# Deeper buffer rings and a new order of all engines in a pre-norm attention and FFN kernel

## The chip, the cores and the metric

The kernel runs on one core of a Trainium2 chip. The metric is device time in microseconds (us). The kernel before took 173.91 us (median of three runs, 173.37 to 174.36). The core's engines are TensorE (PE, with its weight load PEld), VectorE (DVE), ScalarE (ACT) and GpSimd (POOL); SyncE (SP) issues nearly all DMAs.

## The reference

The input x is (32, 256, 128) in float32: 32 sequences of 256 rows, 128 features, 8 heads of 16. One layer is computed:

```
h  = layernorm(x)
q, k, v, g = h @ Wq.T, h @ Wk.T, h @ Wv.T, h @ Wg.T
q, k = rope(q), rope(k)
kv, ksum, vsum = sum_s k_s v_s, sum_s k_s, sum_s v_s     # per head
num = (q @ kv) * scale + vsum;  den = (q . ksum) * scale + S
o  = num / den + depthwise_conv5(v) + bias               # conv over s
x2 = x + (o * g) @ Wo.T
h2 = layernorm(x2) in bfloat16, divided by s_in, rounded to fp8 e4m3
out = x2 + (h2_fp8 @ W_fp8) * (s_in * s_k) + ffn_bias
```

## The kernel before

The work is cut into 16 units (U) of two sequences each, that is 512 rows as four tiles of 128 (TPU). Every unit goes through the same stages, and each engine executes its share in an order that is written out by hand, one call per stage and unit; so several units are in flight at once, and an engine that waits for one stage holds up whatever stands behind it in its own list. Ordering between engines is by counting semaphores: a stage waits for its inputs, and for the reader of the buffer that it overwrites.

The path of one unit u:

- SP `load_x`: x from HBM into `xs` (256 KB, a ring of NX = 4 units). It waits until `residual(u - 4)` has read the slot.
- DVE `stats1`, ACT `var_eps1`, POOL `pow1`, ACT `norm1`: the first layer norm, giving `h`. PE `transpose_h`, ACT `move_hT`: its transpose `hT`.
- PE `project_q`, `project_k`, `project_v`, `project_g` (L1260, L1269, L1279, L1287) from hT. DVE `turn_q_unit` (L968) and `turn_k_unit` (L980) multiply q and k by cosines and sines. SP `swap_q` (L271, L272) moves the two halves of q across partitions with two DMAs, and POOL `add_q` (L700) adds, giving `qT`. POOL `add_k` (L707) gives `k`.
- ACT `move_v`, PE `transpose_v`, ACT `conv_middle` and `conv_outer`, DVE `conv_tap` three times (L995), POOL `sum_outer`: the convolution in `acc`.
- PE `key_value` (L1305), DVE `mask_kv` (L1006), PE `sum_v` and `attend` (L1324), DVE `invert` and `divide`, PE `transpose_t1` (L1333), DVE `add_lepe` (L1030) and `gate`, PE `project_o` (L1343), DVE `residual` (L1047) giving `x2`.
- DVE `stats2`, ACT `var_eps2`, POOL `pow2`, ACT `norm2` (L451): `h2` in bfloat16. SP `turn_h2` (L279) transposes it by DMA into `h2T`; ACT `quantise_if_small` (L485) makes `q8`, PE `ffn` (L1385), ACT `move_y`, POOL `add_bias` and `final_sum`, SP `store` (L261). Units 14 and 15 use PE for this transpose.

q, k, v and the other products live in eight PSUM banks that stages share in turns. A PE stage names in its call which reader must have freed its bank; `project_v(1, (q_turned_done, count(0)))` waits until the DVE has read q of unit 0 from the same bank.

Units 5 to 11 run through regular loops (on the DVE `for t in range(5, 12)`, on PE `for t in range(7, 13)`); the first and the last units have orders of their own. SP has one queue, and its list mixes loads, swaps, transposes and stores, each behind its own wait. Three lines decide what is said of it below:

```
if u >= NX: sp.wait_ge(x2_done, count_last(u, NX))      # load_x
sp.wait_ge(q_turned_done, count(u))                     # swap_q
sp.wait_ge(h2_done, count(u))                           # turn_h2
```

Of the kernel before, what the change touches and what calls it, by code (L numbers as in the profile page):

```python
# [5 lines left out]
P = 128  # L6
D = 128
# [15 lines left out]
NX = 4  # L23
# [33 lines left out]
def h2T_count(u):  # L57

    return 16 * (u // 2 + 1)
# [10 lines left out]
def build(nc, x, wq, wk, wv, wg, wo, lepe_w, lepe_b, ffn_w, s_in, s_k, ffn_b,  # L70
          turn_q_c, turn_k_c, ident_c, mask_c, out):
    ctx = ExitStack()
    with ctx:
# [43 lines left out]
        q_turned = sb("q_turned", [P, 2, 2, W])  # L117
        q_swapped = sb("q_swapped", [P, 2, W])
        k_turned = sb("k_turned", [P, 2, TPU, 2, D])
        k = sb("k", [P, 2, TPU, 2, D // 2])  # L120
        v = sb("v", [P, 3, TPU, NW])
        qT = sb("qT", [P, 2, W])
# [8 lines left out]
        x2 = sb("x2", [P, 3, TPU, D])  # L131
# [5 lines left out]
        h2 = sb("h2", [P, 2, TPU, D], BF16)  # L137
        h2T = sb("h2T", [P, 2, W], BF16)
# [4 lines left out]
        ob = sb("ob", [P, 2, TPU, D])  # L143
# [7 lines left out]
        p_kv = bank[4][:, 0:BPU * NW].rearrange("p (j e) -> p j e", j=BPU)  # L151
        p_h2T = bank[2][:, 0:W // 2].bitcast(BF16)
        p_hT = bank[3]
        p_proj = bank[5][:].rearrange("p (t d) -> p t d", t=TPU)
        p_gT = bank[5]
        p_vT = bank[2][:].rearrange("p (j s) -> p j s", j=BPU)
        p_t1T = bank[3]
        p_y = bank[0]
        p_first_hT = [b[:, 0:S] for b in (bank[2], bank[0])]
        p_end_h2T = [b[:, 0:S // 2].bitcast(BF16) for b in (bank[0], bank[1])]  # L160
        p_end_y = [b[:, 0:S].rearrange("p (t d) -> p t d", t=TPB) for b in (bank[5], bank[4])]
        p_end_t1T = [b[:, 0:S] for b in (bank[4], bank[1])]
        p_end_gT = [b[:, 0:S] for b in (bank[5], bank[3])]
        p_end_proj = [b[:, 0:S].rearrange("p (t d) -> p t d", t=TPB) for b in (bank[0], bank[1])]
# [10 lines left out]
        ob_free = [sem(f"ob_free{n}") for n in range(2)]  # L175
# [27 lines left out]
        q_swapped_in = [sem(f"q_swapped_in{n}") for n in range(2)]  # L203
# [26 lines left out]
        h2T_in = [sem(f"h2T_in{n}") for n in range(2)]  # L230
# [18 lines left out]
        def _(sp):  # L249
# [7 lines left out]
            def store(u):  # L257
                if not 0 <= u < LAST:
                    return
                sp.wait_ge(ob_done, count(u))  # L260
                sp.dma_start(out_v[u], ob[:, u % 2]).then_inc(ob_free[u % 2], 16)  # L261

            def store_end(j):
                sp.wait_ge(end_ob_done[j], 1)
                half = slice(TPB * j, TPB * (j + 1))
                sp.dma_start(out_v[LAST][:, half], ob[:, LAST % 2, half]).then_inc(ob_free[LAST % 2], 16)

            def swap_q(u):
                s = u % 2
# [4 lines left out]
            def turn_h2(u):  # L274
                s = u % 2
# [24 lines left out]
            load_x(3)  # L300
            swap_q(0)
            swap_q(1)
            load_x(4)
# [3 lines left out]
            load_x(5)  # L307
            turn_h2(1)
            for t in range(6, 7):
                load_x(t)  # L310
                swap_q(t - 2)
                turn_h2(t - 4)
                store(t - 5)
            load_x(7)
            store(0)
            swap_q(5)
            turn_h2(3)
            load_x(8)
            store(2)
            swap_q(6)  # L320
            turn_h2(4)
            load_x(9)
            swap_q(7)
            turn_h2(5)
            store(4)
            load_x(10)
            swap_q(8)
            store(3)
            turn_h2(6)
            load_x(11)  # L330
            store(5)
            swap_q(9)
            turn_h2(7)
            store(6)
            swap_q(10)
            load_x(12)
            turn_h2(8)
            swap_q(11)
            store(7)
            load_x(13)  # L340
            turn_h2(9)
            load_x(14)
            swap_q(12)
            load_x(15)
            swap_q(13)
            store(8)
            turn_h2(10)
            turn_h2(11)
            swap_q(14)
            store(9)  # L350
# [10 lines left out]
            sp.wait_ge(ob_free[0], 16 + 16 * (U // 2))  # L361
            sp.wait_ge(ob_free[LAST % 2], 16 + 16 * (U // 2) + 16)

        @block.scalar
        def _(act):
# [79 lines left out]
            def norm2(u):  # L445
                s = u % 2
                act.wait_ge(nmr2_done, count_last(u))
                if u >= 2:
                    act.wait_ge(h2T_in[s], h2T_count(u - 2))
                for t in range(TPU):  # L450
                    last = nc.scalar.activation(h2[:, s, t], x2[:, u % 3, t], ACT.Identity, scale=rs2[:, s, t:t + 1],  # L451
# [3 lines left out]
            def end_norm2():  # L455
                s = LAST % 2
                act.wait_ge(nmr2_done, count_last(LAST, j=0))
                act.wait_ge(h2T_in[s], h2T_count(LAST - 2))
                for t in range(TPB):
                    last = nc.scalar.activation(h2[:, s, t], x2[:, LAST % 3, t], ACT.Identity,  # L460
# [17 lines left out]
            def quantise_if_small(u, is_small):  # L478
                with act.If(is_small == 1):
                    if u < PE_H2:  # L480
                        act.wait_ge(h2T_in[u % 2], h2T_count(u))
# [3 lines left out]
                    nc.scalar.activation(q8[:, u % 2], h2T[:, u % 2] if u < PE_H2 else p_h2T, ACT.Copy, scale=rsc[:, 0:1],  # L485
# [14 lines left out]
            move_hT(0, 1)  # L500
            var_eps1(1)
            move_v(0)
            var_eps1(2)
            norm1(1)
            conv_outer(0)
            conv_middle(0)
            move_hT(1)
            var_eps1(3)
            move_v(1)
            norm1(2)  # L510
            move_hT(2)
            conv_outer(1)
            conv_middle(1)
            norm1(3)
            move_hT(3)
            move_v(2)
            conv_outer(2)
            conv_middle(2)
            var_eps2(0)
            var_eps1(4)  # L520
            move_v(3)
            norm2(0)
            norm1(4)
# [8 lines left out]
            norm2(1)  # L532
            move_v(4)
            var_eps1(5)
            conv_middle(4)
            conv_outer(4)
            quantise_if_small(1, is_small)
            norm1(5)
# [3 lines left out]
            norm2(2)  # L542
            move_v(5)
            var_eps1(6)
            conv_middle(5)
            conv_outer(5)
            quantise_if_small(2, is_small)
            norm1(6)
            var_eps2(3)
            move_y(2)  # L550
            move_hT(6)
            norm2(3)
            move_v(6)
            var_eps1(7)
            conv_middle(6)
            conv_outer(6)
            quantise_if_small(3, is_small)
            norm1(7)
            var_eps2(4)
            move_y(3)  # L560
            move_hT(7)
            norm2(4)
            move_v(7)
            var_eps1(8)
            conv_middle(7)
            conv_outer(7)
            quantise_if_small(4, is_small)
            norm1(8)
            round_identity()
            var_eps2(5)  # L570
            move_y(4)
            move_hT(8)
            for t in range(9, 12):
# [9 lines left out]
                move_hT(t)  # L583
            norm2(8)
            move_v(11)
            var_eps1(12)
            conv_outer(11)
            conv_middle(11)
            quantise_if_small(8, is_small)
            norm1(12)  # L590
# [3 lines left out]
            var_eps1(13)  # L594
            norm2(9)
            norm1(13)
            move_hT(13)
            move_v(12)
            quantise_if_small(9, is_small)
            var_eps2(10)  # L600
            var_eps1(14)
# [991 lines left out]
```

## Time and profile before

| | |
|---|---|
| median of three runs | 173.91 us |
| profiled execution: its own time | 173.71 us |
| its span, first to last instruction | 171.9 us |
| PE busy | 153.9 us (90%) |
| DVE busy | 150.1 us (87%) |
| POOL busy | 136.3 us (79%) |
| ACT busy | 126.3 us (73%) |
| DMA queue of SP and ACT | 33.9% of 16 DMA engines |

The span is 1.81 us shorter than the profiled execution's own time. An engine is busy from the start of an instruction to its end, overlaps counted once; the rest of the span it waits. A row of the timeline gives the start, the duration (of one, or of the merged run when it says x2 or more), the engine, the line, and what is written and read; in square brackets stands the idle time just before it and who ended it.

### The profile page before, as it was taken

How to read it: one execution, taken by the hardware profiler on the slowest of the kernel's cores; microseconds unless marked ns; L12 is line 12 of the kernel's file. 1: busy time of each engine (PE TensorE's matmuls, PEld its weight loads, DVE VectorE, ACT ScalarE, POOL GpSimd, SP SyncE). 2: the span in 40 equal slices, each digit the busy share in tenths (PEclk: the TensorE clock that was granted, in tenths of full speed). 3: DMA queues.
4: the chain of work that ended last, by engine and by line, in shares of the span. 5: the costliest groups of instructions: out<-in, count | busy, mean ns of one | idle time of the engine just before them, and what ended most of it. 6: DMA issues, size and time to landing. Idle time of an engine off the chain costs nothing.

```text
span 171.9 us, 3695 instructions
## 1 busy us (share of the span) xinstructions
PE 153.9 (90%) x1052; PEld 124.9 (73%) x1052; DVE 150.1 (87%) x281; ACT 126.3 (73%) x342; POOL 136.3 (79%) x163
## 2 busy tenths in 40 slices
PE   7789999999899999979999999997999799987620
PEld 2378898877688888858887989857787587965400
DVE  2279899999999999978999999969999959999663
ACT  3757783697889888598889798856798686583851
POOL 1436988858989999969889898969499796979970
PEclk9999999999999999999999999999999999999985
DMA  4932022133133616131552552341508050323223
GB/s 126 280 84 61 4 63 80 44 63 95 31 122 95 185 31 185 34 122 34 153 124 68 144 128 74 72 131 36 123 2 214 5 129 26 97 60 93 66 64 114
DMA packets 29286, 15.74 MB, mean 92 GB/s; under 512 B 9680, under 2 KB 26960, under 8 KB 29264
## 3 DMA queue, kind: packets, MB, share of 16 engines
q1 hardware_dynamic: 28688, 15.22, 33.9%
q10 hardware_dynamic: 576, 0.26, 0.6%
q8 instruction: 9, 0.15, 0.4%
q14 instruction: 13, 0.11, 0.2%
HBM read 5.25 MB, written 4.19 MB: 55 GB/s over the span
## 4 chain that ended last, share of the span: by engine, by line
DVE 23%; PE 22%; DMA 17%; issue 14%; POOL 10%; SPq 7%; ACT 5%; DVEq 0%; POOLq 0%; ACTq 0%
DMA xs<-_attn_hidden_states_dram 6%; DVE acc L995 6%; DMA h2T<-h 5%; DMA q_swapped<-q_turned 5%; DVE k_turned L980 4%; PE bank L1305 4%; DVE x L1047 3%; PE bank L1287 3%; DMA w_raw<-in_L_attn_Wo_dram 3%; POOL rs L671 3%; PE bank L1279 3%; DVE st L958 2%; ACT h L451 2%; PE bank L1269 2%; POOL ob L730 2%
## 5 line engine op out<-in xcount | busy, mean ns | idle before, releaser
L995 DVE SCALAR_TENSOR_TENSOR acc<-bank,conv_w,acc 128x510 f32<-128x510 f32 (+1 forms) x48 | 34.7, 722 | 0.1
L393 ACT ACTIVATE h<-xs,nmr,rs 128x128 f32<-128x128 f32 x64 | 26.3, 483 | 1.7 <-POOL nmr L663 1.5
L451 ACT ACTIVATE h<-x,nmr,rs 128x128 bf16<-128x128 f32 x60 | 24.7, 482 | 3.9 <-POOL nmr L674 3.3
L660 POOL TENSOR_TENSOR rs<-ve,minus_half 128x4 f32<-128x4 f32 (+1 forms) x17 | 16.7, 981 | 10.0 <-ACT ve L384 10.0
L671 POOL TENSOR_TENSOR rs<-ve,minus_half 128x4 f32<-128x4 f32 (+1 forms) x17 | 16.6, 978 | 8.7 <-ACT ve L442 8.6
L700 POOL TENSOR_TENSOR qT<-q_turned,q_swapped 128x512 f32<-128x512 f32 x16 | 20.4, 1277 | 3.4 <-DMA q_swapped<-q_turned 3.4
L1343 PEld LDWEIGHTS bank<-w_o,oT 128*128 128x128 f32 x128 | 16.3, 191 | 7.8 <-issue 4.0
L707 POOL TENSOR_TENSOR k<-k_turned 128x512 f32<-128x512 f32 x16 | 20.4, 1275 | 1.8 <-DVE k_turned L980 1.8
L716 POOL TENSOR_TENSOR acc<-acc,outer 128x508 f32<-128x508 f32 x16 | 20.3, 1271 | 0.6 <-DVE acc L995 0.6
L980 DVE TENSOR_TENSOR k_turned<-bank,turn_k 128x1024 f32<-128x1024 f32 x16 | 19.5, 1218 | 1.3 <-PE bank L1269 1.3
L1305 PEld LDWEIGHTS bank<-v,k 128*128 128x128 f32 x128 | 16.6, 190 | 4.4 <-issue 2.9
L968 DVE TENSOR_TENSOR q_turned<-bank,turn_q 128x1024 f32<-128x1024 f32 x16 | 19.4, 1215 | 0.1
L1343 PE MATMUL bank<-w_o,oT 128*128 128x128 f32 x128 | 17.4, 277 | 2.3 <-DVE oT L1039 2.3
L723 POOL TENSOR_TENSOR yc<-yb,fb 128x512 bf16<-128x512 bf16 x15 | 17.4, 1158 | 1.4 <-ACT yb L492 1.4
L1279 PE MATMUL bank<-w_v,hT 128*128 128x128 f32 x128 | 17.2, 277 | 1.0 <-ACT hT L405 0.7
L1324 PEld LDWEIGHTS p_num<-kvs,qT 128*128 128x128 f32 x128 | 16.8, 190 | 1.7 <-POOL qT L700 0.8
L1305 PE MATMUL bank<-v,k 128*128 128x136 f32 x128 | 17.8, 282 | 0.0
L730 POOL TENSOR_TENSOR ob<-x,yc 128x512 f32<-128x512 f32 x15 | 17.4, 1162 | 0.4
L1279 PEld LDWEIGHTS bank<-w_v,hT 128*128 128x128 f32 x128 | 15.7, 192 | 2.8 <-issue 1.6
L1324 PE MATMUL p_num<-kvs,qT 128*128 128x136 f32 x128 | 17.6, 279 | 0.0
L1316 PE MATMUL p_num<-w_v,hsum 128*128 128x272 f32 x64 | 17.4, 394 | 0.1
L1287 PE MATMUL bank<-hT,w_g 128*128 128x512 f32 (+1 forms) x34 | 16.8, 576 | 0.5 <-DVE x L1047 0.4
(90 smaller groups left out, 338.3 us busy)
## 6 DMA issues: line engine op xcount, KB each, us to landing
q_swapped<-q_turned SPq DMA_DIRECT2D x32, 128.0 KB, 2.8
xs<-_attn_hidden_states_dram SPq DMA_DIRECT2D x15, 256.0 KB, 3.2
out_dram<-ob SPq DMA_DIRECT2D x15, 256.0 KB, 2.9
xs<-_attn_hidden_states_dram SPq DMA_DIRECT2D x2, 128.0 KB, 2.8
turn_q<-in_turn_q_dram SPq DMA_DIRECT2D x1, 256.0 KB, 4.1
turn_k<-in_turn_k_dram SPq DMA_DIRECT2D x1, 256.0 KB, 4.3
out_dram<-ob SPq DMA_DIRECT2D x2, 128.0 KB, 1.8
h2T<-h SPq DMA_TRANSPOSE x14, 2.4
```

The source lines that it names most:

```text
L393: last = nc.scalar.activation(h[:, s, t], xs[:, u % NX, t], ACT.Identity, scale=rs1[:, s, t:t + 1], bias=nmr1[:, s, t:t + 1])
L451: last = nc.scalar.activation(h2[:, s, t], x2[:, u % 3, t], ACT.Identity, scale=rs2[:, s, t:t + 1], bias=nmr2[:, s, t:t + 1])
L671: nc.gpsimd.tensor_tensor(rs2[:, s, part], ve2[:, s, part], minus_half[:, part], ALU.pow).then_inc(pow2_done, 1)
L700: nc.gpsimd.tensor_tensor(qT[:, s], q_turned[:, s, 0], q_swapped[:, s], ALU.add).then_inc(qT_done, 1)
L730: nc.gpsimd.tensor_tensor(ob[:, s], x2[:, u % 3], yc[:, s], ALU.add).then_inc(ob_done, 1)
L980: nc.vector.tensor_tensor(k_turned[:, s].rearrange("p (j a) h d -> p j a h d", j=BPU), p_k.rearrange("p (j a) d -> p j a d", j=BPU).unsque ...
L995: nc.vector.scalar_tensor_tensor(out=part, in0=p_vT[:, :, lo + off:hi + off], scalar=conv_w[:, k:k + 1], in1=part, op0=ALU.mult, op1=ALU.a ...
L1279: last = nc.tensor.matmul(p_v[:, t], hT[:, u % 3, t * P:(t + 1) * P], w_v[:, 0:D], start=True, stop=True)
L1287: nc.tensor.matmul(p_gT[:] if j is None else p_end_gT[j], w_g[:], hT[:, u % 3, part_of(j)], start=True, stop=True).then_inc(gT_filled, 1)
L1305: last = nc.tensor.matmul(p_kv[:, t // TPB], k[:, u % 2, t].rearrange("p a d -> p (a d)"), v[:, u % 3, t], start=(t % TPB == 0), stop=(t % ...
L1324: last = nc.tensor.matmul(p_num[:, t, 0:NW], qT[:, u % 2, t * P:(t + 1) * P], kvs[:, u % 2, t // TPB], start=False, stop=(t % TPB == TPB - 1))
L1343: last = nc.tensor.matmul(dst[:, n], oT[:, u % 2, t * P:(t + 1) * P], w_o[:], start=True, stop=True)
```

## The change

Buffers: `xs` grows from 4 to 6 slots, `x2` from 3 to 4, and `q_turned`, `q_swapped`, `k`, `qT`, `h2`, `h2T` and `ob` from 2 to 3. The waits that protect a slot look back as many units further. PSUM banks are dealt out anew: k, v and the FFN's product share one bank (before: q, v and the FFN's product); q shares one with the transposes of h (before: the transpose of t1 shared that one); kv, the transpose of v and the transpose of t1 have a bank each.

The orders of all five engines are new. In the regular loop little moves: PE projects q before k, and the DVE turns q before k, where it was k before q. The first five units and the last five have other orders. No arithmetic is added or removed.

```diff
-NX = 4
+NX = 6
-        q_turned = sb("q_turned", [P, 2, 2, W])
+        q_turned = sb("q_turned", [P, 3, 2, W])
...
-        p_q = bank[0]
-        p_k = bank[1][:].rearrange("p (t d) -> p t d", t=TPU)
+        p_q = bank[3]
+        p_k = bank[0][:].rearrange("p (t d) -> p t d", t=TPU)
...
             def turn_h2(u):
-                s = u % 2
+                s = u % 3
                 sp.wait_ge(h2_done, count(u))
-                if u >= 2:
-                    sp.wait_ge(q8_done, count(u, 2))
+                if u >= 3:
+                    sp.wait_ge(q8_done, count(u, 3))
...
             def add_k(u):
                 s = u % 2
                 pool.wait_ge(k_turned_done, count(u))
-                if u >= 2:
-                    pool.wait_ge(kv_filled, count(u, 2))
+                if u >= 3:
+                    pool.wait_ge(kv_filled, count(u, 3))
...
# PE, regular loop
-                transpose_t1(t - 3, (hT_done, count_first(t - 1)))
+                transpose_t1(t - 3, (t2_done, count_last(t - 4)))
                 project_v(t - 1, (yb_done, count(t - 5)))
-                project_k(t - 1, (k_turned_done, count(t - 2)))
+                project_q(t - 1, (hT_done, count_first(t - 1)))
                 transpose_v(t - 1, (tap_done[-1], count(t - 2)))
-                project_q(t - 1, (v_done, count(t - 1)))
+                project_k(t - 1, (v_done, count(t - 1)))
...
-                ffn(t - 4, is_small, (q_turned_done, count(t - 1)))
-                transpose_h(t, (t2_done, count_last(t - 3)))
+                ffn(t - 4, is_small, (k_turned_done, count(t - 1)))
+                transpose_h(t, (q_turned_done, count(t - 1)))
```

The first place is PE at the start of the program, from the first projection of k or q on. The rows before (one projection of q is L1260, of k L1269, of v L1279, of g L1287; the transposes of v, h are L1295, L1252; L1305 is key_value, L1316 sum_v):

```order
L1269 MATMUL bank<-w_qk,hT 128x128 x4
L1260 MATMUL bank<-hT,w_qk 128x512
L1316 MATMUL p_num<-w_v,hsum 128x2x136 x2
L1295 MATMUL bank<-ident,v 128x128 x4
L1287 MATMUL bank<-hT,w_g 128x512
L1252 MATMUL bank<-ident,h 128x128 x4
L1305 MATMUL bank<-v,k 128x136 x4
L1279 MATMUL bank<-w_v,hT 128x128 x4
L1269 MATMUL bank<-w_qk,hT 128x128 x4
```

And now (the same functions stand 15 lines further down: q L1275, k L1284, v L1294, g L1302; transposes of v, h L1310, L1267; key_value L1320, sum_v L1331):

```order
L1275 MATMUL bank<-hT,w_qk 128x512
L1310 MATMUL bank<-ident,v 128x128 x4
L1284 MATMUL bank<-w_qk,hT 128x128 x4
L1331 MATMUL p_num<-w_v,hsum 128x2x136 x2
L1302 MATMUL bank<-hT,w_g 128x512
L1267 MATMUL bank<-ident,h 128x128 x4
L1284 MATMUL bank<-w_qk,hT 128x128 x4
L1320 MATMUL bank<-v,k 128x136 x4
L1275 MATMUL bank<-hT,w_qk 128x512
L1294 MATMUL bank<-w_v,hT 128x128 x4
```

Unit 0's q and its transpose of v now stand ahead of its k; unit 1's k ahead of key_value of unit 0, and unit 1's v last, where it was ahead of unit 1's k.

The second place is SP's queue around the loads of the last units. Before, from the load of x for unit 13 to the transposes of h2 for units 10 and 11 (the three loads are units 13, 14 and 15; the transposes 9, then 10 and 11; the swaps 12 and 13; the store 8):

```order
L255 DMA xs<-in_L_attn_hidden_states_dram 128x4x128
L279 DMA_TRANSPOSE h2T<-h 128x4x128
L255 DMA xs<-in_L_attn_hidden_states_dram 128x4x128
L271 DMA q_swapped<-q_turned 64x512
L272 DMA q_swapped<-q_turned 64x512
L255 DMA xs<-in_L_attn_hidden_states_dram 128x4x128
L271 DMA q_swapped<-q_turned 64x512
L272 DMA q_swapped<-q_turned 64x512
L261 DMA out_dram<-ob 128x4x128
L279 DMA_TRANSPOSE h2T<-h 128x4x128 x2
```

And now, from the transpose of unit 8 to that of unit 10 (transposes 8, 9 and 10; swaps 11, 12 and 13; the load of unit 15; stores 7 and 8):

```order
L279 DMA_TRANSPOSE h2T<-h 128x4x128
L271 DMA q_swapped<-q_turned 64x512
L272 DMA q_swapped<-q_turned 64x512
L255 DMA xs<-in_L_attn_hidden_states_dram 128x4x128
L261 DMA out_dram<-ob 128x4x128
L271 DMA q_swapped<-q_turned 64x512
L272 DMA q_swapped<-q_turned 64x512
L279 DMA_TRANSPOSE h2T<-h 128x4x128
L261 DMA out_dram<-ob 128x4x128
L271 DMA q_swapped<-q_turned 64x512
L272 DMA q_swapped<-q_turned 64x512
L279 DMA_TRANSPOSE h2T<-h 128x4x128
```

The loads have moved up: those of units 13 and 14 now stand ahead of this piece, unit 15's ahead of the swap of unit 12, and between the transpose of unit 9 and that of unit 10 there is no load any more; with six slots they wait for x2 of units 7, 8 and 9 where they waited for 9, 10 and 11.

## Rows read from the trace of the kernel before

**Rows 1.** Stretches: start:end, length, then busy us of each engine
```profile
core 0: us, PE busy (x) PEld busy (x) DVE busy (x) ACT busy (x) POOL busy (x), PEclk, DMA share, GB/s
...
60.00:70.00 10.00, 10.00 (x77) 8.84 (x76) 9.96 (x20) 8.74 (x25) 9.54 (x11) 1.00 0.33 93
20.00:110.00 90.00, 87.70 (x625) 74.44 (x624) 87.83 (x156) 74.17 (x200) 79.59 (x90) 1.00 0.34 91
110.00:160.00 50.00, 45.52 (x316) 36.96 (x314) 44.14 (x85) 34.43 (x93) 41.40 (x45) 1.00 0.35 86
160.00:172.00 12.00, 3.25 (x24) 1.94 (x24) 6.82 (x13) 5.58 (x15) 6.21 (x8) 0.75 0.26 74
```

**Rows 2.** DVE timeline, one unit of the regular loop
```profile
59.20 0.68 DVE L1030 TENSOR_TENSOR t<-bank,acc 128x512 f32<-128x512 f32 x1
...
62.28 1.23 DVE L968 TENSOR_TENSOR q_turned<-bank,turn_q 128x1024 f32<-128x1024 f32 x1
...
68.00 0.68 DVE L1030 TENSOR_TENSOR t<-bank,acc 128x512 f32<-128x512 f32 x1
```

**Rows 3.** PE timeline, the same unit
```profile
58.98 1.06 PE L1279 MATMUL bank<-w_v,hT 128*128 128x128 f32 x8
...
61.22 1.02 PE L1260 MATMUL bank<-hT,w_qk 128*128 128x512 f32 x2
```

**Rows 4.** DVE timeline: the larger waits after 70 us, and q_turned of unit 13
```profile
77.84 0.44 DVE L1006 TENSOR_TENSOR kvs<-bank,mask 128x272 f32<-128x272 f32 x1 [1.32 <-PE bank L1305]
...
114.55 0.76 DVE L958 BATCH_NORM_STATS2 st<-xs 128x6 f32<-128x256 f32 x2 [1.43 <-DMA xs<-_attn_hidden_states_dram]
...
122.88 0.76 DVE L958 BATCH_NORM_STATS2 st<-xs 128x6 f32<-128x256 f32 x2 [0.41 <-DMA xs<-_attn_hidden_states_dram]
123.56 1.21 DVE L968 TENSOR_TENSOR q_turned<-bank,turn_q 128x1024 f32<-128x1024 f32 x1
...
139.90 0.69 DVE L1047 TENSOR_TENSOR x<-bank,xs 128x512 f32<-128x512 f32 x1 [1.25 <-PE bank L1343]
141.27 0.19 DVE L1012 TENSOR_SCALAR den<-p_num 128x32 f32<-128x32 f32 x1 [0.67 <-PE p_num L1324]
```

**Rows 5.** SP's queue, 111 to 138 us
```profile
111.36 0.55 SPq L255 DMA_DIRECT2D xs<-_attn_hidden_states_dram  x1
...
128.38 0.38 SPq L255 DMA_DIRECT2D xs<-_attn_hidden_states_dram  x1
128.80 0.52 SPq L271 DMA_DIRECT2D q_swapped<-q_turned  x1
...
130.00 0.60 SPq L261 DMA_DIRECT2D out_dram<-ob  x1
130.70 7.96 SPq L279 DMA_TRANSPOSE h2T<-h  x2
```

**Rows 6.** ACT timeline: waits for the transposed h2, and norm2 of unit 10
```profile
73.05 0.72 ACT L485 ACTIVATE q<-h2T,rsc 128x512 fp8e4<-128x512 bf16 x1 [1.48 <-DMA h2T<-h]
...
127.55 1.64 ACT L451 ACTIVATE h<-x,nmr,rs 128x128 bf16<-128x128 f32 x4
...
134.87 0.72 ACT L485 ACTIVATE q<-h2T,rsc 128x512 fp8e4<-128x512 bf16 x1 [2.10 <-DMA h2T<-h]
```

**Rows 7.** All transposes of h2, from issue to landing
```profile
DMA to landing us min/median/max: 2.4/2.4/4.1
```

**Rows 8.** PE timeline at the start
```profile
15.79 1.16 PE L1279 MATMUL bank<-w_v,hT 128*128 128x128 f32 x8
...
19.59 0.60 PE L1252 MATMUL bank<-ident,h 128*128 128x128 f32 x4
```

**Rows 9.** DVE timeline at the start
```profile
11.39 1.23 DVE L980 TENSOR_TENSOR k_turned<-bank,turn_k 128x1024 f32<-128x1024 f32 x1
...
17.88 1.23 DVE L980 TENSOR_TENSOR k_turned<-bank,turn_k 128x1024 f32<-128x1024 f32 x1 [0.83 <-PE bank L1269]
...
31.39 0.74 DVE L995 SCALAR_TENSOR_TENSOR acc<-bank,conv_w,acc 128x510 f32<-128x510 f32 x1
```

More of the change, by code:

```diff
@@ L541, in _ @@
             move_y(1)
[L542 to L573, printed above, removed]
+            for t in range(6, 9):
                 norm2(t - 4)
@@ L736, in _ @@
             pow1(2)
+            pow1(3)
             add_q(0)
-            pow1(3)
             add_k(1)
@@ L762, in _ @@
             sum_outer(4)
[L763 to L777 removed]
+            for t in range(7, 12):
                 add_k(t - 2)
@@ L1107, in _ @@
             invert(2)
+            stats1(5)
+            divide(2)
             conv_tap(3, 1)
-            divide(2)
+            mask_kv(3)
+            add_lepe(2)
             conv_tap(3, 2)
-            for t in range(5, 12):
+            gate(2)
+            turn_q_unit(4)
+            turn_k_unit(4)
+            quantise_if_wide(1, is_small)
+            residual(2)
+            conv_tap(4, 0)
+            stats2(2)
+            invert(3)
+            conv_tap(4, 1)
+            divide(3)
+            conv_tap(4, 2)
+            for t in range(6, 11):
                 mask_kv(t - 2)
@@ L1476, in _ @@
+            project_k(11, (v_done, count(11)))
+            transpose_v(11, (tap_done[-1], count(10)))
+            project_o(9, (oT_done, count_last(9)))
+            sum_v(10, (t1_done, count_last(9)))
+            transpose_h(12, (q_turned_done, count(11)))
+            attend(10)
+            ffn(8, is_small, (k_turned_done, count(11)))
             project_g(10, (x2_done, count_last(9)))
+            project_q(12, (hT_done, count_first(12)))
             key_value(11, (kvs_done, count(10)))
-            transpose_t1(10, (hT_done, count_first(12)))
+            project_v(12, (yb_done, count(8)))
@@ L1485, in _ @@
[L1485 to L1492 removed]
+            project_k(13, (k_turned_done, count(12)))
+            key_value(12, (kvs_done, count(11)))
@@ L1493, in _ @@
+            project_q(13, (hT_done, count_first(13)))
+            transpose_t1(11, (t2_done, count_last(10)))
+            sum_v(12, (t1_done, count_last(11)))
+            ffn(9, is_small, (k_turned_done, count(13)))
+            attend(12)
+            project_g(11, (x2_done, count_last(10)))
+            project_v(13, (yb_done, count(9)))
+            transpose_h(14, (q_turned_done, count(13)))
             project_o(11, (oT_done, count_last(11)))
-            sum_v(12, (t1_done, count_last(11)))
@@ L1495, in _ @@
-            project_v(13, (yb_done, count(9)))
-            transpose_h(14, (t2_done, count_last(11)))
-            attend(12)
+            key_value(13, (kvs_done, count(12)))
             transpose_v(13, (tap_done[-1], count(12)))
-            project_q(14, (v_done, count(13)))
+            transpose_t1(12, (t2_done, count_last(11)))
+            sum_v(13, (t1_done, count_last(12)))
+            ffn(10, is_small, (v_done, count(13)))
             project_g(12, (x2_done, count_last(11)))
-            project_k(14, (k_turned_done, count(13)))
```

570 lines of the change are left out of this document (299 added, 271 removed).

## Prediction

> **What bounds the kernel now.** I read the stretches first, then one unit of the loop on the DVE and on PE, then the waits inside the timelines, and last SP's own queue, since most of what the change touches is when a transfer is issued.
>
> The stretches [rows 1] show two engines that are full at once. From 60 to 70 us PE is busy 10.00 of 10 us and the DVE 9.96. One unit costs the DVE 68.00 - 59.20 = 8.80 us [rows 2] without a wait in it, and the change adds and removes no arithmetic, so the loop cannot run faster than that. POOL has 9.54 of 10 us and ACT 8.74; neither has much to spare. The granted clock of PE is 1.00 until 160 us, which is the 2.4 GHz level, and 0.75 on average in the last stretch. So time can come only from three places: the start, the waits in between, and the end.
>
> How much is there in between: from 20 to 110 us the DVE idles 90 - 87.83 = 2.2 us, of which one wait is 1.32 us [rows 4]. From 110 to 160 us it idles 50 - 44.14 = 5.9 us and PE 50 - 45.52 = 4.5 us [rows 1]. That last part is where the units' orders leave the regular loop, and it is the target of this sum. PE's 4.5 us is also a lid on it: the DVE cannot gain more there than PE can follow, since PE's work has to be done as well.
>
> **The change part by part.**
>
> Loads of x (six slots). Two DVE waits after 20 us are for x: 1.43 us (unit 13) and 0.41 us (unit 14) [rows 4]. Unit 13's load was issued at 111.36 [rows 5] and the DVE reached its statistics at 114.55 - 1.43 = 113.12, so 1.43 us of the 3.2 from issue to use were not covered. With four slots the load waits for x2 of unit 9; with six it waits for x2 of unit 7, two units or some 17.6 us earlier, and in SP's list it stands ahead of the swap of unit 10. Even where the statistics of units 13 and 14 are moved up by several DVE calls, over 3 us of cover are left. The gain is between 0 (another wait takes its place) and 1.84 us; I take 1.6.
>
> Transposes of h2 stuck behind loads. Unit 10's h2 was ready at 127.55 + 1.64 = 129.2 [rows 6], but its transpose was issued at 130.70, because SP stood at the load of unit 15 until 128.38 (waiting for x2 of unit 11), and then had to issue the swap of unit 13 and the store of unit 8 [rows 5]. That swap's data was ready at 123.56 + 1.21 = 124.8 [rows 4]; it stood 4 us behind a load. The transpose then landed in 4.1 us, where the median is 2.4 [rows 7], ACT waited 2.10 us for it [rows 6], and PE and the DVE felt it: the DVE waits of 1.25 and 0.67 us at 139.90 and 141.27 [rows 4] stand in that wake, behind ffn, project_v and project_o of the following calls. In the new list no load is between the transposes of units 9 and 10, and the load of unit 15 waits for x2 of unit 9. The swap of unit 13 is still just ahead of the transpose of unit 10. Between 0 and 1.92 us; I take 1.3, since a swap of 256 KB in all may still be in its way.
>
> The Trainium skill says in "DMA: Bandwidth & Descriptors", section "Queues, rings and completion order", that SP's DMAs use one ring on each of the 16 DMA engines and that each engine takes descriptors in ring order. The trace agrees for the 4.1 us at 130.70, which followed three transfers in 2 us. By that rule the new list, which puts the swaps of units 13 and 14 right ahead of the transposes of units 10 and 11, would again bring late landings, and this term would be 0 (time 171.7). That is a rival below.
>
> The other waits from 110 to 160 us. 5.9 - 1.84 - 1.92 = 2.1 us of DVE idle are left, in pieces of 0.1 to 0.7 us. The order there is new in every engine. Between 0 and 2.1 us, and since a new order brings its own small waits I take 0.5.
>
> The loop itself (q before k). PE's and the DVE's second place of the pair now belongs to k, where it was q's. The DVE started on the second of the two at 62.28, and PE had ended it at 61.22 + 1.02 = 62.24 [rows 2, 3]. k takes four matmuls and ends some 0.03 us later than q did. At most 0.1 us a unit, and I take 0. k is turned 1.2 us later (one q_turned, 1.23 [rows 2]), still ahead of its place in POOL's list, behind pow1 and sum_outer; q is turned 1.2 us earlier, so its swap starts earlier, where POOL sometimes waited for it, off the path. The wait of PE's transpose of h moves from t2 to q_turned of the unit before, which now ends where k_turned ended, at 62.28, and PE comes to that transpose after project_o, sum_v, attend and ffn. This costs nothing. The third slots of h2, h2T, qT and k free producers that did not wait for a slot in this loop, and the DVE's 9.96 of 10 us leaves no room for a gain: 0.
>
> The wait of 1.32 us at 77.84 [rows 4] comes down from ACT's 1.48 us wait for the transposed h2 at 73.05 [rows 6]. That landing was late too. In the loop ACT keeps its order (norm2, then move_v, var_eps1, conv_middle, conv_outer, quantise), so its cover stays what it was. Nothing here is cured. It may be absent (-1.3) or come again elsewhere (+1.3 each time); I take 0.
>
> The start. PE now runs project_q and the transposes of v ahead of unit 0's project_k: one q (1.02 us [rows 3]) and four transposes (0.60 us [rows 8]), overlapped about 1.3 us. So k_turned of unit 0 moves from 11.39 [rows 9] to about 12.7, and with it add_k and key_value. On the DVE q_turned of unit 0 fills the hole. From 11.39 to the end of the first tap of unit 2 at 31.39 + 0.65 = 32.04 the DVE had one clear wait, 0.83 us at 17.88 [rows 9]. Walking the new list with the same durations I find waits of about 0.1 (turn_k of unit 0), 0.4 (turn_k of unit 1, now behind unit 1's project_k), 0.25 (first tap of unit 1) and 0.2 us of crumbs: 0.95 for the same calls. The cost is +0.1, between -0.5 and the price of the slower rival below.
>
> The end. The last unit's second divide moves ahead of its first add_lepe, and PE's second project_g ahead of ffn(13). From 160 us on the chain is the same: norm, transpose, quantise, ffn, output. I take 0 (-0.4 to +0.3).
>
> The sum against the profiled execution, 173.71 us (span 171.9 and 1.81 around it; the median of the runs is 173.91, 0.2 higher): 173.71 - 1.6 - 1.3 - 0.5 + 0.1 = 170.4. As a check on PE's lid: its 4.5 us of idle from 110 to 160 us would shrink to 1.1.
>
> **The rivals.**
>
> Slower, the start on PE. Before, unit 1's project_v began at 15.79 and the transpose of h of unit 2 at 19.59 [rows 8]. Now the first must wait for k_turned of unit 1 (by hand 18.4) and the second stands behind it, behind attend, transpose_v and key_value (by hand 21.8). For: PE's list is in order, both engines are full from 20 us on, and what is lost at the start comes back nowhere. The parts of the chain are k of unit 0 1.3 us, project_v 2.6, transpose of h 2.2; if they add up instead of overlapping, the loss is 6.1 us, and the time 170.4 - 0.1 + 6.1 = 176.4. It decides against the change from a loss of 4.5 us on. Against: by the DVE's calls the three overlap, and the first statistics of unit 4 stand earlier in the new list, since its x is loaded at once.
>
> The gain is given back. The DVE's waits go, but PE, ACT or POOL has one in the same place: POOL was busy 41.40 of 50 us there [rows 1] and its list is rearranged as well. Only a fifth of the 3.3 us arrives: 173.71 - 0.6 = 173.1, between 172.9 and 174.5.
>
> Late transposes, by ring order. The term of 1.3 us fails and the rest holds: 171.7. Were landings like those two to strike in three more units, each at 1.32 us, it would be 174.4.
>
> More than forecast. All 1.84 + 1.92 + 1.5 of the waits go, and the accident at 77.84 does not happen: 173.71 - 5.3 - 1.3 + 0.1 = 167.2; with PE's lid of 4.5 in place of 5.3 it is 168.0. For: with two engines full, every wait that goes is gained whole.
>
> **How the numbers follow.** Forecast (169.2 to 171.5) 0.45; late transposes 0.10; more gain (167.2 to 169.2) 0.13; given back 0.20; slower at the start 0.12. A difference under 0.5%, that is under 0.87 us on 173.91, can't be told from none here. Faster (under 173.04): 0.45 + 0.10 + 0.13 less 0.03 for tails, and 0.03 of the given-back case: 0.68. Slower (over 174.78): 0.13. Same: 0.19. The predicted time is 170.4. Forecast, late transposes, most of the larger gain and most of the given-back case lie between 167.9 and 174.3; the forecast's own range is 169.2 to 171.5.
>
> **What would show it.** Right: no DVE wait for x after 20 us; SP's transposes of units 9 to 12 issued within 0.5 us of norm2's end; DVE idle from 110 to 160 us down from 5.9 to about 2.5 and PE's from 4.5 to about 1; the first tap of unit 2 ends near 32.1; one loop unit still 8.80 us. Wrong: the tap of unit 2 past 34 us (the start); DVE idle in the last third unchanged with new names of releasers (given back); ACT waiting over 1 us for h2T in two or more units.

## The result and the profile after

The changed kernel takes 168.0 us (median of four runs, 167.9 to 168.3). The kernel before, run beside it, takes 173.6. The ratio is 0.967, with a 95% interval from 0.964 to 0.971. The forecast was 170.4 with a range from 167.9 to 174.3, so the direction was right, the time lies at the lower edge of the range, and the gain was 5.6 us where 3.5 had been forecast. It lies outside the forecast's own range of 169.2 to 171.5, in that of the case of more gain, which had been given a chance of 0.13.

The stretches of the profiled execution after (168.33 us, span 166.5), to be set against [rows 1]:

```profile
60.00:70.00 10.00, 10.00 (x73) 8.25 (x72) 9.97 (x20) 8.93 (x25) 9.50 (x11) 1.00 0.28 66
20.00:110.00 90.00, 89.38 (x644) 75.44 (x642) 88.65 (x161) 73.81 (x202) 80.80 (x92) 1.00 0.38 93
110.00:160.00 50.00, 45.09 (x323) 37.06 (x321) 46.01 (x89) 37.31 (x101) 44.81 (x49) 0.98 0.32 79
```

The loop is as full as before. From 20 to 110 us PE (first figure behind the length) idles 0.6 us in place of 2.3 and the DVE (third) 1.35 in place of 2.2. From 110 to 160 us the fixed window now takes in 5 us of the end, so there I compare by landmarks: from the DVE's residual of unit 9 to the first half of that of unit 15. Before, these stood at 109.46 and 160.82, after at 108.90 and 155.13. The waits in between (the stretch less the engine's busy time in it) fell from 5.91 to 1.95 us on the DVE and from 4.66 to 1.91 on PE. Those left are small:

```profile
116.81 1.23 DVE L967 TENSOR_TENSOR k_turned<-bank,turn_k 128x1024 f32<-128x1024 f32 x1 [0.26 <-PE bank L1284]
125.23 0.69 DVE L1026 TENSOR_TENSOR oT<-bank,t 128x512 f32<-128x512 f32 x1 [0.37 <-issue]
131.31 0.69 DVE L1026 TENSOR_TENSOR oT<-bank,t 128x512 f32<-128x512 f32 x1 [0.22 <-issue]
144.69 0.19 DVE L999 TENSOR_SCALAR den<-p_num 128x32 f32<-128x32 f32 x1 [0.22 <-PE p_num L1339]
```

All five waits of [rows 4] are gone, also the one at 77.84, which no part of the change was seen to cure. SP's queue, against [rows 5]:

```profile
116.57 1.44 SPq L279 DMA_TRANSPOSE h2T<-h  x1
...
124.16 0.60 SPq L272 DMA_DIRECT2D q_swapped<-q_turned  x1
125.58 1.21 SPq L279 DMA_TRANSPOSE h2T<-h  x1
127.62 0.38 SPq L261 DMA_DIRECT2D out_dram<-ob  x1
```

The last load of x is gone from this stretch, and unit 10's transpose is issued at 125.58, as its norm2 ends:

```profile
119.47 0.72 ACT L486 ACTIVATE q<-h2T,rsc 128x512 fp8e4<-128x512 bf16 x1 [0.80 <-DMA h2T<-h]
...
123.92 1.64 ACT L452 ACTIVATE h<-x,nmr,rs 128x128 bf16<-128x128 f32 x4
...
128.13 0.72 ACT L486 ACTIVATE q<-h2T,rsc 128x512 fp8e4<-128x512 bf16 x1 [0.46 <-DMA h2T<-h]
...
139.49 0.72 ACT L486 ACTIVATE q<-h2T,rsc 128x512 fp8e4<-128x512 bf16 x1 [0.97 <-DMA h2T<-h]
```

ACT still waits for three landings, 2.2 us in all where four had cost 5.1 before, but no wait of the DVE there is above 0.4 us. The landings themselves, against [rows 7]:

```profile
DMA to landing us min/median/max: 2.4/2.5/3.5
```

One by one, the transposes of units 9, 10 and 11 landed 2.8, 2.5 and 3.5 us after their issue.

What bounds the kernel now is said most plainly by the chain of waits, where PE had 22% before:

```profile
PE 78%; DVE 5%; POOL 5%; issue 4%; SPq 3%; DMA 3%; ACT 1%; POOLq 0%; DVEq 0%; ACTq 0%
```

### The profile page after: what moved, and what is told of

Its sections match the earlier page's. It is cut to its first block, busy times and chain, and to the rows that moved or that the text cites. A ratio compares the mean times of both kernels' runs of the same rounds, so it can differ in the third digit from the quotient of the medians.

```text
span 166.5 us, 3690 instructions
## 1 busy us (share of the span) xinstructions
PE 151.4 (91%) x1052; PEld 123.3 (74%) x1052; DVE 149.5 (90%) x281; ACT 125.9 (76%) x342; POOL 136.1 (82%) x164
## 4 chain that ended last, share of the span: by engine, by line
PE 78%; DVE 5%; POOL 5%; issue 4%; SPq 3%; DMA 3%; ACT 1%; POOLq 0%; DVEq 0%; ACTq 0%
PE bank L1284 9%; PE bank L1275 8%; PE p_num L1331 8%; PE bank L1294 8%; PE bank L1320 8%; PE p_num L1339 8%; PE bank L1358 7%; PE bank L1302 7%; PE bank L1310 4%; PE bank L1348 4%; PE bank L1267 4%; DMA w_raw<-in_L_attn_Wo_dram 3%; DVE acc L982 2%; PE bank L1400 2%; POOL yc L724 1%
## 5 line engine op out<-in xcount | busy, mean ns | idle before, releaser
L1320 PEld LDWEIGHTS bank<-v,k 128*128 128x128 f32 x128 | 16.5, 190 | 3.5 <-issue 3.3
L1284 PE MATMUL bank<-w_qk,hT 128*128 128x128 f32 x128 | 17.1, 276 | 0.9 <-ACT hT L406 0.9
L1294 PEld LDWEIGHTS bank<-w_v,hT 128*128 128x128 f32 x128 | 15.9, 192 | 2.7 <-issue 1.9
L1320 PE MATMUL bank<-v,k 128*128 128x136 f32 x128 | 17.6, 281 | 0.0
L1294 PE MATMUL bank<-w_v,hT 128*128 128x128 f32 x128 | 17.1, 276 | 0.6 <-ACT hT L406 0.6
L1284 PEld LDWEIGHTS bank<-w_qk,hT 128*128 128x128 f32 x128 | 15.7, 192 | 2.4 <-issue 1.2
L1331 PE MATMUL p_num<-w_v,hsum 128*128 128x272 f32 x64 | 17.3, 393 | 0.0
```

Of the source, the lines that this page charges most:

```text
L1284: last = nc.tensor.matmul(p_k[:, t], hT[:, u % 3, t * P:(t + 1) * P], w_qk[:, 1].rearrange("p a d -> p (a d)"), start=True, stop=True)
L1294: last = nc.tensor.matmul(p_v[:, t], hT[:, u % 3, t * P:(t + 1) * P], w_v[:, 0:D], start=True, stop=True)
L1320: last = nc.tensor.matmul(p_kv[:, t // TPB], k[:, u % 3, t].rearrange("p a d -> p (a d)"), v[:, u % 3, t], start=(t % TPB == 0), stop=(t % ...
L1331: nc.tensor.matmul(p_num[:, TPB * j:TPB * (j + 1), 0:NW], hsum[:, u % 3, j:j + 1].to_broadcast([P, P]), w_v[:].unsqueeze(1).to_broadcast([ ...
```

## The experiments

Each was run with the kernel before beside it on the same chip; times are medians, ratios are to that kernel. There were twelve runs.

### Is the wait at 77.84 chance? (the kernel before once more)

> The kernel before, unchanged, profiled a second time. It asks whether the 1.32 us wait of the DVE at 77.84, which came down from a late transpose of h2, belongs to the order or to chance. Theory chance: ACT's waits for the transposed h2 stand in other units, and the DVE's wait near 77.8 is gone or elsewhere; time 172.3 to 174.4. Rival, the order: the same wait of 1.2 to 1.4 us within 0.5 us of 77.8, and all units as before to 0.2 us. The two larger waits for x (1.43 and 0.41 us) and the transpose of unit 10 (landing 4.1 us) come back under both.

173.79 us (one run).

```profile
77.89 0.44 DVE L1006 TENSOR_TENSOR kvs<-bank,mask 128x272 f32<-128x272 f32 x1 [1.43 <-PE bank L1305]
```

The wait stands where it stood, behind ACT's wait for h2T of 1.58 us. It comes in both profiled executions, and in all five kernels below that keep the old lists of the four engines and PE's matmuls as they were, so it belongs to the program. The landing of unit 10's transpose does vary between executions of the same kernel: ACT waited 2.76 us for it here, and 2.10 in [rows 6].

### Six slots of x alone

```diff
-NX = 4
+NX = 6
```

> The kernel before with six slots for x instead of four, nothing else: no list moved. Theory head of line: what cost most is that SP stood at a load. The load of unit 15 no longer waits for x2 of unit 11, the swap of unit 13 and the transpose of unit 10 go out on time, its landing is 2.4 to 2.8 us and not 4.1, and the DVE waits of 1.25 and 0.67 us go; the wait for x of unit 14 goes, that of unit 13 shrinks to about 0.9 us since its load still stands behind the store of unit 7: 173.7 - 1.9 - 0.4 - 0.5 = 170.9. Rival, the orders do it: a ring alone brings under 0.9 us, 172.8 to 173.8.

172.15 us, ratio 0.988 (0.982 to 0.993), between the two times expected. The six slots did something else than I had said. The waits for x stayed:

```profile
114.40 0.76 DVE L958 BATCH_NORM_STATS2 st<-xs 128x6 f32<-128x256 f32 x2 [1.64 <-DMA xs<-_attn_hidden_states_dram]
...
123.56 0.76 DVE L958 BATCH_NORM_STATS2 st<-xs 128x6 f32<-128x256 f32 x2 [1.24 <-DMA xs<-_attn_hidden_states_dram]
```

```profile
111.01 0.55 SPq L255 DMA_DIRECT2D xs<-_attn_hidden_states_dram  x1
...
120.59 1.52 SPq L255 DMA_DIRECT2D xs<-_attn_hidden_states_dram  x1
125.48 0.47 SPq L271 DMA_DIRECT2D q_swapped<-q_turned  x1
```

Load 13 is free to go long before, but it stands in SP's list behind the transpose of unit 8, a swap and a store, and leaves at 111.01, as before at 111.36. What the slots cured is the other stall: load 15 is issued at 120.59 in place of 128.38, nothing stands ahead of unit 10's transpose, and ACT's 2.10 us wait of [rows 6] is gone; its largest for h2T from 80 to 142 us is 0.28.

### All rings, the old orders and banks

The declarations, slot numbers and waits of the changed kernel, with the call lists, SP's list and the banks of the kernel before.

> All rings of the change (x 6, x2 4, q_turned, q_swapped, k, qT, h2, h2T and out 3) under the orders and the PSUM banks of before. Theory: only the ring of x was waited for, so this equals the kernel with six slots for x alone, within 0.4 us (about 170.9). Rival: the small rings matter by themselves (qT, k or h2 free their producers): 0.8 us or more below it.

172.15 us, ratio 0.988 (0.982 to 0.993), beside the last one on the same chip, and equal to it as the theory had it. The DVE waits 1.48 and 1.66 us for x, and 1.38 at 77.79. Beside x, the third slots give these orders nothing.

### All rings and SP's new list, the other orders old

> All rings, and SP's list of the change; the lists of PE, DVE, ACT and POOL and the banks as before. Theory: SP's list brings what is left of the waits for x (0.9 us) and nothing else: 170.0 to 170.4. If the lists of the four engines carry the rest of the 5.6 us, this stays 2 us above the changed kernel (168.0). Rival: the rings and SP's list are the whole gain, and it reaches 168.5 or less.

175.04 us, ratio 1.004 (1.001 to 1.008): 0.4% slower than before, and 2.9 us above the last one. The expectation, 170.0 to 170.4, was wrong by 4.6 us. The waits for x after 110 us are gone (one of 0.37 us stands at 87.90), but now the list asks for stores and swaps in an order in which the old lists of POOL and the DVE do not make them ready, and SP stands at each with a transpose behind it:

```profile
136.23 0.38 SPq L261 DMA_DIRECT2D out_dram<-ob  x1
136.66 0.51 SPq L271 DMA_DIRECT2D q_swapped<-q_turned  x1
137.21 0.60 SPq L272 DMA_DIRECT2D q_swapped<-q_turned  x1
137.91 1.23 SPq L279 DMA_TRANSPOSE h2T<-h  x1
```

```profile
140.56 0.72 ACT L486 ACTIVATE q<-h2T,rsc 128x512 fp8e4<-128x512 bf16 x1 [3.51 <-DMA h2T<-h]
```

ACT had ended the norm of that unit by 134.42, 3.5 us before the transpose was issued. The DVE then waited 3.06 us at 143.94. SP's list and the engines' lists are one piece.

### Rings, old orders, two loads of x moved up

```diff
             load_x(12)
+            load_x(13)
             turn_h2(8)
             swap_q(11)
+            load_x(14)
             store(7)
-            load_x(13)
             turn_h2(9)
-            load_x(14)
             swap_q(12)
```

> All rings with the old lists (172.15), and in SP's list only the loads of units 13 and 14 moved up: 13 ahead of the transpose of unit 8, 14 ahead of the store of unit 7. Theory: the DVE's waits for x (1.48 and 1.66 us in that kernel) are a matter of place in SP's list; both go, and with PE and the DVE both full before and after, most of the 3.1 us arrives: 169.3 to 170.3. Rival: PE cannot follow and the lists of the four engines have to change as well; under 1 us comes, 171.2 or more.

169.76 us, ratio 0.973 (0.968 to 0.979). No wait for x after 20 us; the largest DVE waits left up to 150 us are 1.38 us at 77.77 and 0.67 at 113.82. So the place of two loads is worth 2.4 us once there are six slots, and the old orders come within 1.8 us of the changed kernel (167.96 with six idle instructions in it, on the same chip). The wait at 77.77 is 1.38 of these, so all the rest of the new orders can be worth some 0.4 us.

### The new orders, all rings but that of x at their old sizes

The changed kernel with two slots of q_turned, q_swapped, qT, k, h2, h2T and ob, and three of x2.

> The kernel after, with the rings other than that of x at their old sizes (q_turned, q_swapped, qT, k, h2, h2T and the output 2, x2 3); orders, banks and the six slots of x are the new ones. Theory (the new orders bring the gain, the rings only have to be there for x): within 0.5 us of the changed kernel, 167.6 to 168.6, DVE idle between residual(9) and residual(15) under 2.5 us. Rival (each new order was written for a third slot, so that a producer or SP now waits for one): waits of POOL for q_turned/qT or of SP for h2T in units 9 to 14 over 0.5 us, time 169.5 to 172.

168.14 us, ratio 0.965 (0.961 to 0.968), the same as the changed kernel. So no ring but that of x matters for the time under the new orders. Whether they need the six slots of x was not run.

### The wait at 77.84: thirty-two idle instructions at PE's head, six in the changed kernel

```diff
+            for _ in range(32):
+                pe.nop(nofuse=True)
             pe.wait_ge(zero_set, 1)
```

> The kernel before, with 32 empty instructions at the head of PE's list, while PE waits for its first data. Nothing else moves. In every kernel with the old lists the transpose of h2 for unit 4 landed in 4.0 us or more and the DVE waited 1.3 to 1.4 us near 77.8; its 512 data packets were on time (2.0 to 2.8 us after issue) and a 16 KB packet of queue 8, kind instruction, ran from 2.8 to 3.7 us. Theory: that packet is PE's own next block of instructions, and one of the transpose's 16 completion writes stands behind it on one DMA engine. 32 instructions more move the block some 2 us earlier, ahead of the transpose: landing 2.4, no DVE wait at 77.8, and 1.3 us less: 172.4 (against 173.7), unless the shift brings the block onto another transpose. Rival: the lateness belongs to the transpose or its neighbours in SP's list; then it stays, and the time is 173.5 to 174.0.

173.85 us, ratio 0.999 (0.995 to 1.002). What gave the idea was the record of the single packets. In the kernel before, the transpose of unit 4 is issued at 68.94; its 512 packets of data run from 1.19 to 1.97 us after that, as those of other units do. It ends with 32 packets of 4 bytes, two for each of the 16 increments of the semaphore by which it reports that it is done. Thirty of them start by 2.06 us, two at 2.83 and 2.84. A packet of 16 KB on the queue that brings instructions starts at 1.97 and takes 0.88 us, so it ends at 2.85. The DMA view has the packet between 70.90 and 70.95:

```profile
q8 instruction: 1, 0.02, 109.9%
```

and between 71.00 and 71.80 nothing starts but the two late reports, both after 71.70:

```profile
q1 hardware_dynamic: 2, 0.00, 2.8%
```

Fifteen of the 16 increments came by 2.48 us after the issue, the last at 4.02. The expectations above and below put all these packets 0.8 us too late (data from 2.0 to 2.8, packet from 2.8 to 3.7 us after the issue); the distances between the packets hold.

The idle instructions did not do their work: the packet stood at 70.8 in place of 70.9, 1.97 us after the issue as before, the wait stayed at 1.39 us, and so the run tells nothing on the theory.

> The changed kernel with 6 empty instructions at the head of PE's list, some 0.4 us of PE's stream. In it the instruction blocks of queue 8 start 3.0 and 3.1 us after the issue of the transposes of units 4 and 7, whose completion writes end at 2.7 us: a narrow miss. Theory: moved 0.4 us up, one or both blocks catch a completion write, that transpose lands in 3.5 to 4.2 us, ACT waits 1.0 us or more, and the time is 0.8 to 2.5 us above 168.0: 168.8 to 170.5. Rival: the time does not depend on such a shift, 167.8 to 168.2.

167.96 us, ratio 0.964 (0.958 to 0.969). The packet started 2.19 us after the transpose's issue (2.22 in the changed kernel), still past the start of the last report at 2.08, and nothing changed. My expectation of a hit failed.

### Instructions that do move the packet

```diff
-            keep_busy(p_gT, 13)
+            keep_busy(p_gT, 11)
+            for _ in range(40):
+                nc.tensor.matmul(p_gT[:, 0:1], zero[:, 0:P], zero[:, 0:1], start=True, stop=True)
```

> The kernel before, with 11 matmuls of zeros at its head in place of 13, and 40 matmuls of one column behind them: PE's instruction stream is 38 matmuls longer, its time at the head about the same. Theory (the transpose of unit 4 lands late since one of its completion writes stands behind a 16 KB packet that brings instructions): if the packet near 71.7 us moves earlier by more than 1 us, the transpose lands 2.4 us after its issue, the DVE's wait of 1.3 us at 77.8 is gone, and the time is 172.4. Rival (the late landing has to do with the order of SP's transfers alone): wait stays at 1.3 to 1.4 us and the time at 173.6. If the packet does not move, neither is told apart.

The packet moved from 70.9 to 65.3 us, the reports of unit 4's transpose all started by 2.06 us after its issue, and the wait was gone:

```profile
76.34 0.74 DVE L995 SCALAR_TENSOR_TENSOR acc<-bank,conv_w,acc 128x508 f32<-128x508 f32 x1
76.99 0.43 DVE L1006 TENSOR_TENSOR kvs<-bank,mask 128x272 f32<-128x272 f32 x1
```

The time did not fall: 175.46 us (173.9 to 176.3), ratio 1.005 (0.999 to 1.010). The cause of the wait is confirmed, and my 172.4 was wrong. In the profiled execution (174.34 us) the 1.3 us were given back at two places; the median lies 1.1 us above it, and what made the other executions slower no trace shows. The store ahead of unit 13's load stood like this in the kernel before:

```profile
110.73 0.58 SPq L261 DMA_DIRECT2D out_dram<-ob  x1
```

and like this here, with the load behind it:

```profile
109.48 1.61 SPq L261 DMA_DIRECT2D out_dram<-ob  x1
111.13 0.50 SPq L255 DMA_DIRECT2D xs<-_attn_hidden_states_dram  x1
```

```profile
114.26 0.76 DVE L958 BATCH_NORM_STATS2 st<-xs 128x6 f32<-128x256 f32 x2 [2.40 <-DMA xs<-_attn_hidden_states_dram]
```

```profile
135.70 0.72 ACT L485 ACTIVATE q<-h2T,rsc 128x512 fp8e4<-128x512 bf16 x1 [3.31 <-DMA h2T<-h]
```

The DVE reached unit 13's statistics 1.3 us earlier, but the load left only 0.23 us earlier. The store ahead of it took 1.61 us to issue in place of 0.58. An instruction packet started at 109.44, and whether it held up the issue no run tells. Unit 10's transpose, issued at 130.30, landed in 5.3 us, and ACT waited 3.31 us for it in place of 2.10. An instruction packet came at 131.36, but all 16 increments were late, and the kernel before had 4.1 and 4.8 us in its two profiles without such a packet there. So what part the packet had in this wait is not shown.

> The rings with the old orders and the loads of x for units 13 and 14 moved ahead in SP's list (169.8 us before), with the same 38 matmuls more at PE's head. Theory (instruction packet): the wait at 77.8 goes here too, 168.4 us, so the old orders reach the changed kernel within 0.5 us. Rival (the wait is of the order): 169.8.

170.09 us (169.2 to 170.9), ratio 0.978 (0.972 to 0.983). The same edit on the rings with the two loads moved up. Again the wait at 77.8 was gone, and again another came, this time behind the swap of q, issued at 107.01 and 107.52, with the packet at 108.97. Of the 32 increments of the two transfers one came 1.6 us behind the others:

```profile
111.53 1.27 POOL L701 TENSOR_TENSOR qT<-q_turned,q_swapped 128x512 f32<-128x512 f32 x1 [2.13 <-DMA q_swapped<-q_turned]
```

Without the edit POOL waited 0.54 us there. ACT's norm2 then waited 2.44 us for POOL, PE 0.87 and the DVE 1.13 (at 120.79). Net, nothing was gained: the expected 168.4 did not come.

### The packet put onto a landing, in the changed kernel

```diff
             keep_busy(p_gT, 13)
+            for _ in range(4):
+                nc.tensor.matmul(p_gT[:, 0:1], zero[:, 0:P], zero[:, 0:1], start=True, stop=True)
```

> The kernel after, with 4 matmuls of one column behind those of zeros at PE's head (some 0.1 us of work, before any data is there). 38 such matmuls had moved PE's instruction packet from 71.7 to 66.1 us, so 4 move it some 0.6 us, from 3.0 to about 2.4 us after the issue of unit 4's transpose, onto its landing. Theory (where the packet falls decides, and the new orders only happened to miss it): the transpose lands some 3.7 to 4.1 us after its issue, ACT waits 1.0 to 1.5 us for it near 72, the DVE 1.0 to 1.4 us near 77, and the time is 168.9 to 169.4. Rival (the new orders are robust, or the packet doesn't hold up a landing): 167.9 to 168.2, no wait over 0.3 us between 70 and 80 us.

169.48 us (169.2 to 169.7), ratio 0.978 (0.974 to 0.983), against 168.0 and 0.967 without these four instructions. The transpose of unit 4 was issued at 69.07, and the packet came at 71.02, 1.95 us after the issue where it had been 2.22 in the changed kernel, and ended at 2.83. The data ran until 1.95 in both. Thirty of the 32 reports started by 2.04, two at 2.81 and 2.82:

```profile
DMA to landing us min/median/max: 4.0/4.0/4.0
```

```profile
73.17 0.72 ACT L486 ACTIVATE q<-h2T,rsc 128x512 fp8e4<-128x512 bf16 x1 [1.53 <-DMA h2T<-h]
```

```profile
77.96 0.44 DVE L993 TENSOR_TENSOR kvs<-bank,mask 128x272 f32<-128x272 f32 x1 [1.34 <-PE bank L1320]
```

This is the wait of the kernel before, in the same place and size. Four instructions, 0.24 us of PE's time in all, cost 1.5 us (1.9 by the ratios). That the packet misses is luck of the new lists and no merit of them.

The same reading settles unit 11's landing of 3.5 us in the changed kernel, for which ACT waited 0.97 us at 139.49. Its increments came by 2.44 us after the issue at 135.92, save one at 3.48. Here the packet has 8 KB and is on another queue of the kind "instruction"; the view from 137.70 to 137.85 has it:

```profile
q14 instruction: 1, 0.01, 36.7%
```

It starts 1.85 us after the issue and ends at 2.73; the last two reports start at 2.73 and 2.74.

### The changed kernel with the end's second norm on ACT

```diff
                 last.then_inc(end_h2_done[0], 1)
+                act.wait_ge(nmr2_done, count_last(LAST))
+                for t in range(TPB, TPU):
+                    last = nc.scalar.activation(h2[:, s3, t], x2[:, LAST % 4, t], ACT.Identity,
+                                                scale=rs2[:, s, t:t + 1], bias=nmr2[:, s, t:t + 1])
+                last.then_inc(end_h2_done[1], 1)
```

(and the DVE's call of end_norm2 goes)

> The changed kernel, with the second half of the last unit's norm2 done by ACT instead of the DVE. On the DVE its two instructions take 1258 ns each beside POOL's add_bias, on ACT the same tile takes 483 ns. Theory: the last chain (norm, transpose, quantise, FFN, output) of the second half starts its transpose 0.8 us earlier, and the kernel ends 0.6 to 0.9 us earlier: 167.1 to 167.4. Rival: ACT's quantise of the first half now stands behind the second half's norm, and what is won is lost there, 167.8 to 168.3.

166.96 us, ratio 0.958 (0.954 to 0.962), faster than both kernels. The changed kernel has the first row, this one the second:

```profile
158.87 2.38 DVE L878 TENSOR_SCALAR h<-x,rs,nmr 128x128 bf16<-128x128 f32 x2 [1.90 <-POOL nmr L675]
```

```profile
158.69 0.87 ACT L466 ACTIVATE h<-x,nmr,rs 128x128 bf16<-128x128 f32 x2
```

Two tiles take the DVE 2.38 us and ACT 0.87. POOL runs two instructions beside the DVE's, from 158.79 to 159.94 and from 160.02 to 161.17, and the DVE's two tiles end at 160.02 and 161.25, each 0.08 us after one of them. The Trainium skill says in "SBUF — State Buffer", section "SBUF: two separate sides", that GpSimd and a VectorE instruction in a two-port mode take a shared pair of ports as an exclusive lock, which the one that starts first holds for its whole instruction. The trace agrees for the first tile, which starts after POOL's instruction and ends just behind it. The second starts 0.07 us ahead of POOL's and lasts 1.31 us all the same, so it does not fit plainly. No run here took the POOL instructions away, so the cause is not shown.

## Why the prediction was right, and where it was too small

By landmarks, the two profiled executions differ by 5.4 us of span, which splits into -0.13 at the start, +1.37 in the regular loop, +3.96 in the last third, -0.3 at the end, and 0.5 of instructions that read shorter. The prediction had -0.1, 0, +3.4, 0 and 0.

**The start** came out as walked. PE's transpose of h for unit 2 stands at 21.79 us and unit 1's project_v at 18.61, later than in [rows 8] by what had been said (21.8, 18.4), and the DVE's first k_turned is at 12.72 (12.7):

```profile
18.61 1.05 PE L1294 MATMUL bank<-w_v,hT 128*128 128x128 f32 x8
...
21.79 0.60 PE L1267 MATMUL bank<-ident,h 128*128 128x128 f32 x4
```

The parts overlapped, and the slower rival fell. The mark at 32.1 us for the tap of unit 2 was no good: in the new list that tap stands ahead of other calls and starts at 29.16.

**x, 1.6 us.** Right in size, half right in mechanism. I had put it down to the slots and to SP's list together. The slots alone left both waits (1.64 and 1.24 us); with two loads moved up they went, for 2.4 us. Slots are the permission, the place in the list is the act.

**Transposes of h2, 1.3 us.** Right: issued within 0.1 us of norm2's end for units 9 to 11. What cured it was the six slots, alone worth some 2 us (172.15 against 174.19 beside it), since SP no longer stands at load 15. The size was too low: I kept 0.6 us back for the swap ahead of the transpose. The rival of late transposes named ring order as the cause, and that did not come: unit 10's transpose, issued 1.4 us behind the second half of a swap, landed in 2.5 us, the median. Unit 9's took 2.8, and unit 11's 3.5 behind an instruction packet. ACT's waits of 0.80, 0.46 and 0.97 us for them hardly reached the DVE. The rival's 174.4 is also a slip: three more units at 1.32 us on its own 171.7 make 175.7.

**The other waits, 0.5 us.** The last third gave 3.96 us, 0.56 more than the three terms together. Not told apart by a run; the DVE's 1.95 us that are left lie below the 2.5 forecast.

**The wait at 77.84, taken as 0.** This is the term that was wrong by most. I called it an accident that "may be absent (-1.3) or come again elsewhere". It is no accident: in seven kernels and executions with the old orders of the engines and the packet in its place it measures 1.32 to 1.43 us, and it is a transfer whose report stands behind an instruction packet. Its going is some 1.3 us of the 2.1 by which the gain was short, and so nearly a quarter of the measured gain is luck. The price of both sides was right, the chance of each could not have been read from the views I used; it was in the packets' records.

**The loop and the rings, 0.** Right: 8.78 us a unit in place of 8.80, and the kernel with small rings runs at 168.14.

**PE's lid.** The likeliest case left 1.1 us of PE's waits; 1.91 are left by landmarks. The nearest rival, more than forecast with PE's lid, named 168.0 and the two parts that made it: the waits of the last third, and the absence of the one at 77.84. It too met the number in part by luck: it counted 4.5 us in the last third, where 3.96 went, and took the absence for an accident.

Open: the end is 0.3 us longer (11.37 against 11.08 from the first half of the last residual on), with a granted clock of 0.64 in place of 0.75 from 160 us on, and no run was spent on it.

## What to carry to other kernels

More slots for a loaded tile do not cure the waits for that tile if its load stands behind waiting instructions in its queue; look for the issue time in the queue's own rows, move the load up, and price the two edits apart. A queue's order is worth only as much as the orders of the engines that make its data ready: SP's new list under the old orders of the engines cost 2.9 us. Where one wait comes back in each execution in a loop that is otherwise regular, look at the single packets of its transfer before calling it chance, and don't credit a new order with its absence: an edit of four instructions can bring it back. Six slots and two lines moved in SP's list gave most of what the new orders of five engines gave; price such a small edit first.

## What the runs showed of the hardware

Instructions arrive over DMA queues of their own while the kernel runs: nine packets of 16 KB on one queue in a run of 170 us here (ten with 38 matmuls more), each of 0.88 to 1.76 us, and packets of 8 KB on another. A transfer with a report behind such a packet is late: 4.0 us from issue to landing in place of 2.4, and 1.3 to 1.4 us on the DVE when both engines are full. The Trainium skill says in "DMA: Bandwidth & Descriptors", section "Queues, rings and completion order", that the semaphore's increment lands only after every earlier write from that DMA engine, across its queues. The trace agrees: the two late reports start at 2.83 and 2.84 us, where the instruction packet ends at 2.85. It does not account for all of it: these reports start 0.8 us late and the last increment comes 1.6 us late, and no packet of the trace shows where the other 0.8 us go.

What decides is where the packet starts. Over the profiles of all kernels here, in all fourteen cases in which an instruction packet started 1.81 to 1.97 us after the issue of a transpose of h2, one increment came 0.65 to 1.65 us behind the others. Where it started between 2.19 and 2.7 us after the issue and the data were on time, none did.

That the packets of 16 KB are PE's is worked out: 38 matmuls more, each with its weight load, moved one by 5.6 us. Thirty-two idle instructions in PE's list moved it by no more than 0.1 us, and why is open.
